# Waiting for the fourth gather behind in place of the third, in a four-layer graph network kernel

## The reference, cut to what matters

```python
xs = s[dst]
xv = v[dst]
out0a = w0 * xs
...
tp = jnp.concatenate([out0a, out0b, out1a.reshape(E, -1), out1b.reshape(E, -1), out1c.reshape(E, -1)], axis=-1)
agg = jax.ops.segment_sum(tp, src, num_segments=N) / DENOM
```

## Time and profile before

| | us |
|---|---|
| median of three runs | 5657.94 |
| lowest and highest | 5654.71, 5666.39 |
| the profiled execution, its own time | 5651.99 |
| its span, first to last instruction | 5650.1 |
| setup, until the first gather | 1126 |
| gathers of layer 0 | 1126.3 to 2277.3 |
| gathers of layer 1 | 2409.9 to 3414.6 |
| gathers of layer 2 | 3488.4 to 4482.9 |
| gathers of layer 3 | 4573.0 to 5576.0 |

### The profile page before, as it was taken

One profiled execution on the slowest core, in us unless ns is written; L12 is line 12 of the kernel. 1 busy time (PEld: TensorE's weight loads), 2 busy tenths in 40 slices (PEclk: granted clock), 3 DMA queues, 4 the chain that ended last, 5 costly groups with the idle time before them and its releaser, 6 DMA issues.

```text
span 5650.1 us, 105356 instructions
## 1 busy us (share of the span) xinstructions
PE 4324.1 (77%) x24426; PEld 3349.4 (59%) x24426; DVE 3529.2 (62%) x11475; ACT 3412.2 (60%) x14606; POOL 4001.4 (71%) x4336
## 2 busy tenths in 40 slices
PE   7795122099999999889999997555565788888998
PEld 5553011066666676777788886444444666666777
DVE  8896000177777777667777887333333477777888
ACT  0000000066666565478889997677778777788886
POOL 5777777777777777467777775777777557777775
PEclk8898555599999999989999998555555599999999
DMA  9625553144444444133333332333333223333332
GB/s 316 182 76 117 111 126 88 50 92 91 91 90 91 90 91 91 29 77 79 80 80 80 81 80 54 78 79 79 80 81 81 63 62 79 79 79 80 80 81 54
DMA packets 632976, 504.27 MB, mean 89 GB/s; under 512 B 424230, under 2 KB 538341, under 8 KB 630454
## 3 DMA queue, kind: packets, MB, share of 16 engines
q0 software_dynamic: 183824, 307.52, 21.7%
q1 hardware_dynamic: 430566, 156.52, 12.0%
q10 hardware_dynamic: 17984, 33.56, 1.6%
HBM read 400.41 MB, written 96.88 MB: 88 GB/s over the span
## 4 chain that ended last, share of the span: by engine, by line
issue 26%; POOL 25%; PE 15%; DMA 6%; DVE 5%; DVEq 1%; ACT 1%; SPq 0%; POOLq 0%; ACTq 0%
POOL gath L961 17%; POOL gath L939 8%; DMA gath<-table,rows 3%; PE bank L1948 3%; DMA gath<-table,acc 3%; PE bank L1944 2%; PE bank L1922 2%; PE bank L1998 2%; PE bank L1950 2%; DVE acc L1529 2%; PE bank L1990 1%; DVE work L1563 1%; DVE work L1542 1%; DVE work L1545 1%; ACT sel L1121 1%
## 5 line engine op out<-in xcount | busy, mean ns | idle before, releaser
L961 POOL DMA_INDIRECT gath<-table,acc x2346 | 2221.5, 947 | 819.4 <-issue 674.4
L1121 ACT ACTIVATE sel<-acc,rows 128x32 f32<-128x32 f32 x10560 | 2292.9, 307 | 466.6 <-DVE acc L1520 466.1
L1529 DVE TENSOR_TENSOR acc<-acc,bank 128x160 f32 (+1 forms) x3520 | 1212.6, 344 | 922.5 <-PE bank L1944 574.8
L1948 PE MATMUL bank<-work,sel 128*128 128x160 f32 (+1 forms) x5280 | 1395.2, 346 | 150.7 <-DVE acc L1529 138.3
L1950 PE MATMUL bank<-work,sel 128*128 128x160 f32 x5280 | 1154.9, 300 | 0.0
L1948 PEld LDWEIGHTS bank<-work,sel 128*128 128x128 f32 x5280 | 839.8, 190 | 437.9 <-issue 415.1
L939 POOL DMA_INDIRECT gath<-table,rows x880 | 838.8, 953 | 317.7 <-issue 258.1
L1922 PE MATMUL bank<-w,work 64*128 64x224 f32 (+2 forms) x5280 | 925.3, 370 | 73.2 <-DVE work L1545 55.8
L794 POOL DMA_INDIRECT rows_a<-acc x782 | 755.0, 965 | 280.6 <-issue 237.9
L1950 PEld LDWEIGHTS bank<-work,sel 128*128 128x128 f32 x5280 | 913.2, 191 | 45.9
L1944 PE MATMUL bank<-gath,sel 128*128 x1760 | 564.4, 494 | 425.8 <-POOLq L947 361.5
(11 more groups left out here) (288 smaller groups left out, 3647.9 us busy)
## 6 DMA issues: line engine op xcount, KB each, us to landing
rows<-rows_b SPq DMA_DIRECT2D x330, 128.0 KB
gath<-table,acc POOLq DMA_INDIRECT x2346
rows_a<-acc ACTq DMA_DIRECT2D x1, 30360.0 KB, 103.1
rows<-rows_a SPq DMA_DIRECT2D x110, 256.0 KB
acc<-in_rows_a SPq DMA_DIRECT2D x34, 793.5 KB, 7.2
rows_b<-gath SPq DMA_DIRECT2D x16, 896.0 KB, 10.7
gath<-table,rows POOLq DMA_INDIRECT x880
acc<-in_rows_b SPq DMA_DIRECT2D x34, 368.0 KB, 3.7
```

The lines of the kernel that those rows point to most:

```text
L961: pool.indirect_dma_start(gath_all[:, u, :], None, table_dram[n][:, :], bass.IndirectOffsetOnAxis(ap=index[:, k:k + 1], axis=0)).then_inc( ...
L1121: i = act.activation(sel[q][:, t, at:at + BIN], hot, ACT.Copy, scale=e[:, k:k + 1])
L1529: dve.tensor_tensor(sums, sums, bank(6 + b, P, 256 * h, 256 * h + L.width), ALU.add).then_inc(S["fl"].sem, 1)
L1948: pe.matmul(out, sel[qv][:, t, 96:224], work[:, a + NF:a + NF + L.width], start=True, stop=False, skip_group_check=True)
```

## The change

`IN_FLIGHT` goes from 3 to 4, and an assertion is loosened so that it may equal the number of semaphores. Gather k now waits for the landing of gather k - 4, in all four layers. The increments that tell of a landed half stand with that wait, so they move by one gather too.

```diff
-IN_FLIGHT = 3
+IN_FLIGHT = 4
 LANES = 4
-assert IN_FLIGHT < LANES and GT % LANES == 0 and HALF % LANES == 0
+assert IN_FLIGHT <= LANES and GT % LANES == 0 and HALF % LANES == 0
```

## The result

The changed kernel took 5574.53 us in the median of 5 runs (5567.30 to 5576.78), the kernel before 5659.97 us beside it (5 runs, 5654.71 to 5666.39): a ratio of 0.9847, 95% interval 0.9836 to 0.9858. The profiled execution took 5567.3 us with a span of 5564.6 us, against 5651.99 and 5650.1 before. The forecast was 5563 us, the range 5546 to 5602.

A forecast was written before the change was run, and what follows sets the result against it. POOL's gather streams were taken to bound the kernel; layer gains of 40.7, 20.4, 15.0 and 18.6 us, together 94.7, off the 5657.94 us median gave 5563 us, range 5546 to 5602.

The forecast's parts named there:

- The landing waits go: POOL's gather streams, all layers: idle time waiting for landings, 73.1 us, practically all vanishes with 1.25 us more room.
- their floor: Gather streams at the quiet pace of 1.25 us per gather: 1099.7 us in layer 0, 977.2 in the others.
- the longer gathers: Gathers slower than the quiet 945 ns: 7.0 us in layer 0, 1.6 in each other layer, untouched by the change.
- the 52.9 of the labels: Lower bound of POOL's landing waits, from idle times the profile puts down to a landing: 52.9 us.
- The later arrivals: Listeners hear of landed halves up to 1.25 us later, one shift per layer; costs 1.25 us each in layers 1 and 3.
- The slower rival: Layer 0's row loads issued up to 1.25 us later hold up each group's first gather: up to 5698 us, chance 0.05.
- The pauses: POOL's 28 stops, every 110th gather, 37.0 us over usual idle time: each gives back up to 1.25 us, 29.8 in all.
- the rival in which the pauses stay: Only landing waits go, the stops at every 110th gather remain: 66.7 us gained, 5591 us, chance 0.25.
- Behind the lockstep: Layers 1 and 3: stream gains after some 88% of the stream are worth nothing, as listeners no longer wait for arrivals.
- Layers 0 and 2 pay nothing at their end: Last landings there are waited for directly as before, so later increments cost these two layers 0 us.
- DVE's waits: Layer 0: DVE's waits for arrivals fall from 218 us by about the layer's gain, its work staying the same.
- Nothing: Rival: a fourth gather under way only slows each, so the wait moves and doesn't go: 5658 us, chance 0.08.

The follow-up runs named there:

- Telling late alone: Kernel before, every gather still waiting for the third behind, only the listeners' increments moved one gather later: 5626.67 us, ratio 0.9954 on A.
- the window alone: Kernel before with gathers waiting for the fourth behind, increments left ahead of the third gather behind: 5611.98 us, ratio 0.9929 on A.
- window 6: Changed kernel with gather k waiting for the landing of k - 6, eight landing semaphores, increments two gathers later: 5550.12 us, ratio 0.9818 on A; 7815.91 us on B.
- A: Chip of the follow-up runs without "remote" idle times; the kernel before took 5651.53 us there.
- The extra instruction: Kernel before plus one semaphore increment that nobody waits for in POOL's queue at each gather: 7817.33 us on chip C (one run).
- window 2: Kernel before with gather k waiting for the landing of k - 2: 6748.34 us on A, 7175.55 us on B (one run each).
- windows 6 and 8: The 8: as window 6, but IN_FLIGHT = 8, waits and increments five gathers later than in the kernel before: 7823.24 us, ratio 1.0065 on chip C.
- B and C: Two other chips with long "remote" idle times; the kernel before took 7752.68 us on B and 7765.68 us on C.

## Why the prediction was right, and where its steps were off

**The landing waits go: right.** 73.1 us were to go. What is left that a landing ends is 0.9 us over the usual idle time, and the streams are 13.6, 6.6, 4.7 and 5.5 us over their floor of 1099.7 and 977.2, 30.4 us in all, where the pauses and the longer gathers alone account for that (see the pauses below). Taking the upper bound, 73.1, and not the 52.9 of the labels was right too.

**Why they go: only half of the mechanism.** The prediction reckoned with 1.25 us more for a gather to look. Telling late alone gave 25 us and the window alone 40, so a good part of the 73.1 us (29.7 us stand at one gather in four) was waited for at the increment, where the prediction saw a cost only. The diff was to be read as moving two waits, not one.

**The later arrivals: wrong.** The listeners were to hear of a landed half up to 1.25 us later, at 1.25 us in each of layers 1 and 3. They hear of it when they did before, 2.63 us after the start of the half's last gather where it was 2.64, because POOL's queue runs ahead of its gathers. So these 2.5 us of the sum had no cause. The slower rival took the same delay from the row loads (7.6 us left of 8.9); measured, their room went from 9.1 to 8.6 us in the median.

**The pauses: the step that was mis-sized.** They were to give back up to 1.25 us each, 29.8 of 37.0, and leave 7.2 us. The longer gathers now cost 880 x 0.010 + 3 x 782 x 0.003 = 15.8 us (11.8 before, from the page's rounded means), and 30.4 - 15.8 = 14.6 us are left for the pauses (15.2 by their idle times themselves): they gave back 22. The row at 1417.99 went from 2.21 to 1.86 us only, that at 1705.92 (gather 443 of layer 0) from 1.84 to 1.43, while the first went from 1.78 to 0.58. The premise, that a pause gives back up to 1.25 us, fails on both sides: those at the last gather of a half gave back 0.2 to 0.9 us, and of the others five gave back more, 1.3 to 1.8. Its other half, that a pause needs a queue held back by waits, is supported by window 6 on A, where there is none. By the Trainium skill's "Runtime: NRT & Kernel Launch", section "Instruction fetch mechanics", cited in the prediction for the rival in which the pauses stay, instructions are fetched in blocks of 256, so what it describes would return by a number of instructions. The extra instruction left the pauses 110 gathers apart, so the measurement speaks against it here.

**Shortfall by the sum.** Streams: 102.9 forecast, 91.4 measured, 11.5 short: 7.4 by the pauses (14.6 left in place of 7.2) and 4.0 by the longer gathers (15.8 in place of 11.8).

**Behind the lockstep: the size about right, the reason coarser than told.** Layers 1 and 3 were to lose 4.2 and 4.0 us of their streams' gain at the end, and lost 20.9 - 18.4 = 2.5 and 20.3 - 16.4 = 3.9. In fact the lockstep ends much earlier now: no wait of DVE for an arrival stands behind 3100 us in layer 1 or behind 5200 us in layer 3, some 74% and 71% of the way, where before they went to 3300 and 5470. With no later arrivals, 12% of the stream's gain would be 2.5 and 2.4 us; layer 1 fits that, layer 3 lost more.

**Layers 0 and 2 pay nothing at their end: right.** 37.6 and 37.4, 12.6 and 12.6.

**DVE's waits: wrong in size.** They were to fall by about the layer's gain, and fell by 80 us against 37. The step took DVE's remaining work as fixed; it left out that a DVE whose halves come closer together meets PE, the next one to be late (27.6 us more at L1529 alone).

**The rivals.** The pauses stay (5591): refuted in part, they shrank by 60%. Nothing (5658): refuted. Slower by the row loads: refuted; no gather but the very first waits for a load, with window 6 neither. The time itself, 5574.5 us, lies between the forecast and this first rival, a little nearer to the forecast.

## What to carry to other kernels

In a stream of equal asynchronous transfers, where a queue waits for the landing of the one N behind, compare the room, N pitches of the stream, with the tail of the landings, both from the start of a transfer, and not with their median: 3.75 us against landings of 2.6 us in the median and up to 4.7 let 200 of 3226 gathers wait, 5.0 us let almost none, and a window of 6 cleared what was left, some 15 us more. Count the waits by their place, and those in instructions of their own, such as in front of an increment for a listener, apart from the gathers' own: they may hold the stream up when the others no longer do. And don't take a later place in the queue for a later event: read from the trace when the instruction is done. Before going on, look who is next; here a window of 6 brought PE to 99.7% busy in layer 0, and on chips where the other engines stand still for reasons of their own the same edit gained nothing.

## What the runs showed of the hardware that was not expected

- POOL stands still at every 110th gather, counted in gathers across the layers and not in queue instructions (3117 more of them moved nothing), for up to 3.9 us with window 2 and 2.5 us with window 3. With windows 6 and 8 and eight semaphores it is every 106th gather, for up to 2.2 us on B and C, and nothing is left of it with window 6 on A. The cause is open.
- An increment for a listener that is moved one gather later made the kernel 25 us faster (0.9954, 0.9937 to 0.9971) though no gather waited with more room.
- POOL's queue ran ahead of the gathers it issues, by 4.8 us in the half shown with window 6: increments behind the third, fourth and sixth gather all came 2.63 to 2.64 us after the start of the half's last gather (median of layer 0).
- A gather of 128 rows of 640 bytes landed 2.6 us after its start in the median, one in a hundred after more than 3.8 to 4.0 us, the longest after 4.7, and a fourth gather on its way changed none of it.
- The same program took 5652 us on one chip and 7753 and 7766 on two others, with ACT idle for up to 27 us at a time, DVE for up to 21 and PE for up to 14, put down to "remote". There the denser stream had more of it (863 such idle times with window 6, 229 with window 2), and the order of the versions turned round: window 2 took 7176 us (one run), window 6 7816.
